# Earlier selections, more product buffers and more empty steps in a two-layer convolution kernel

## The reference, cut to what matters

```python
# layer 0: local attention over 3 x 3 neighbours, 4 heads of 64 channels
qkv = einsum('oc,bchw->bohw', w_qkv, gn(x));  q, k_, v = split(qkv, 3)
logits = einsum('bhdl,bhdkl->bhkl', q, patches(k_))            # 9 per pixel and head
attn_out = einsum('bhkl,bhdkl->bhdl', softmax(logits, axis=2), patches(v))
kernel = einsum('hkc,bhcl->bhkl', w_kg_g, cat) + b_kg          # 9 dynamic weights
conv_out = einsum('bhkl,bhdkl->bhdl', kernel, patches(v))
x = x + einsum('oc,bchw->bohw', w_proj, alpha * conv_out + beta * attn_out)
# layer 1: modulated deformable 3 x 3 convolution
om = conv3x3(gn(x), w_off) + b_off                             # offsets and masks
v = bilinear samples of gn(x) at each pixel, for 9 taps, times sigmoid(mask)
x = x + einsum('bckhw,ock->bohw', v, w)
```

## Time and profile before

| | us |
|---|---|
| median of 3 runs | 5400.81 (5400.7 to 5404.68) |
| the profiled execution | 5390.38 |
| its span, first to last instruction | 5388.6 |
| PE busy | 4889.6 (91%) |
| DVE busy | 4392.5 (82%) |
| ACT busy, POOL busy | 2297.6 (43%), 2282.9 (42%) |
| mean granted clock of PE | 0.972 of full speed |

### The profile page before, as it was taken

One profiled execution on the slowest core, in us unless ns is written; L12 is line 12 of the kernel. 1 busy time (PEld: TensorE's weight loads), 2 busy tenths in 40 slices (PEclk: granted clock), 3 DMA queues, 4 the chain that ended last, 5 costly groups with the idle time before them and its releaser, 6 DMA issues. The chain is left out here.

```text
span 5388.6 us, 80437 instructions
## 1 busy us (share of the span) xinstructions
PE 4889.6 (91%) x26816; PEld 2678.9 (50%) x26816; DVE 4392.5 (82%) x11212; ACT 2297.6 (43%) x5430; POOL 2282.9 (42%) x2311
## 2 busy tenths in 40 slices
PE   7868999999989998999989999899998989988888
PEld 4435554555545555455544555445554555544443
DVE  5656888878887888878888788888888878898998
ACT  2234444344443443534445344343444444443554
POOL 0003444444453444434444444444444344454776
PEclk9979999999999999999999999999999999999999
DMA  4326778877798777977779777887778877788999
GB/s 162 122 93 208 271 248 291 304 250 264 247 318 285 251 266 245 337 269 259 257 251 338 250 258 256 277 315 250 275 254 292 297 252 263 251 305 308 387 398 353
DMA packets 493125, 1451.51 MB, mean 269 GB/s; under 512 B 47396, under 2 KB 117420, under 8 KB 492460
## 3 DMA queue, kind: packets, MB, share of 16 engines
q0 software_dynamic: 331776, 1208.11, 64.3%
q1 hardware_dynamic: 160940, 238.27, 12.6%
HBM read 1309.60 MB, written 136.59 MB: 268 GB/s over the span
## 5 line engine op out<-in xcount | busy, mean ns | idle before, releaser
L730 POOL DMA_INDIRECT G<-table,IDX x2304 | 2282.0, 990 | 3066.6 <-DVE V L1381 2269.6
L749 PE MATMUL ps<-VT,s_wconv 128*128 128x512 f32 x4608 | 2277.5, 618 | 39.7 <-DVE R L1165 39.7
L1381 DVE SCALAR_TENSOR_TENSOR V<-G,WT,V 128x256 f32<-128x256 f32 x4608 | 2019.1, 479 | 122.6 <-DVE V L1381 3.2
L1109 ACT ACTIVATE VT<-ps 128x512 f32<-128x512 f32 x1152 | 686.0, 595 | 2390.0 <-PE ps L955 2387.9
L749 PEld LDWEIGHTS ps<-VT,s_wconv 128*128 128x128 f32 x4608 | 828.7, 194 | 871.7 <-issue 836.1
L1374 DVE SCALAR_TENSOR_TENSOR V<-G,WT 128x256 f32<-128x256 f32 x2304 | 1006.5, 477 | 84.0 <-ACT G L1098 40.1
L1129 DVE TENSOR_TENSOR E<-ps,s_band 128x512 f32<-128x512 f32 x1024 | 649.5, 682 | 455.3 <-PE ps L811 273.3
L955 PEld LDWEIGHTS ps<-s_ident,V 128*128 128x128 f32 x4608 | 574.5, 143 | 755.8 <-issue 754.5
L1098 ACT ACTIVATE G<-G,WT 128x256 f32<-128x256 f32 x1850 | 841.2, 499 | 111.0 <-DMA G<-table,IDX 110.1
L955 PE MATMUL ps<-s_ident,V 128*128 128x128 f32 x4608 | 708.8, 277 | 86.4 <-DVE V L1381 84.4
L787 PE MATMUL ps<-XN,s_wqk 128*128 128x512 f32 x1024 | 490.1, 606 | 14.8 <-ACT XN L1011 14.6
(11 more groups left out here) (101 smaller groups left out, 2764.9 us busy)
## 6 DMA issues: line engine op xcount, KB each, us to landing
table<-E SPq DMA_DIRECT2D x384, 176.0 KB
G<-table,IDX POOLq DMA_INDIRECT x2304
X<-in_x SPq DMA_DIRECT2D x64, 512.0 KB, 7.3
x<-X SPq DMA_DIRECT2D x64, 512.0 KB, 7.0
R<-x SPq DMA_DIRECT2D x64, 512.0 KB
out<-R SPq DMA_DIRECT2D x64, 512.0 KB, 5.8
G<-in_x SPq DMA_DIRECT2D x56, 512.0 KB, 4.4
s_wconv<-in_wconv SPq DMA_DIRECT2D x1, 2304.0 KB, 9.2
```

The costliest lines, as they stand in the source:

```text
L730: e.indirect_dma_start(G[a % NG][:, :], None, T[b % 2], bass.IndirectOffsetOnAxis(ap=IDX[b % 2][:, col:col + 1], axis=0)).then_inc(d_g[a % ...
L749: mm = e.matmul(CV[oh][:, :], s_wconv[:, h, t, oh * P:(oh + 1) * P], VT[U % 2][:, h, :], start=(t == 0 and h == 0), stop=(t == 8 and h == 1))
L1109: e.activation(VT[U % 2][:, :, 2 * P * pair:2 * P * (pair + 1)], BK[banks.place[use]][:, :].rearrange("p (h n) -> p h n", h=2), ACT.Copy). ...
L1381: e.scalar_tensor_tensor(vt[:, :], gt[:, q * C:(q + 1) * C], wt[:, col, q:q + 1], vt[:, :], ALU.mult, ALU.add).then_inc(lerp[q - 1], 1)
```

## The change

- `NE_BUF` goes from 4 to 6 (each buffer is 128 x 1024 float32, 4 KB per partition).
- `scores`: `hop(COLLECT)`, three empty steps, instead of one ahead of `ext`; and `hop(TURN)`, two, between `lg.out` and `lt`.
- `mix`: the first heads' `sel` waits only for x1 of chunk c - 1; the second heads' `sel` waits for the logits of chunk c + 1; both pairs of `sel` come before the first `pv`, and each `pv` has `hop(1 + alone)` ahead of it.
- `IDX` and `WT` become one tile each for nine chunks (`NW` = 9), addressed by `column(b, c, i, t)`; `w.mix` waits for the blending nine chunks back, from the tenth chunk on.
- the small tile `row` moves into a part of `G[3]`.

```diff
-NE_BUF = 4
+NE_BUF = 6
+NW = 9
+COLLECT, TURN = 3, 2
@@ def scores
-        yield IDLE
+        yield from hop(COLLECT)
         yield ("ext", b, c)
         have_logits.add((b, c))
         yield ("lg.out", b, c)
+        yield from hop(TURN)
         yield ("lt", b, c)
@@ def mix
-        while c > 0 and (b, c - 1) not in have_x1 or c + 1 < NCH and (b, c + 1) not in have_logits:
+        while c > 0 and (b, c - 1) not in have_x1:
             yield IDLE
         for hp in range(2):
+
+            while hp == 1 and c + 1 < NCH and (b, c + 1) not in have_logits:
+                yield IDLE
             for of in (OWN, BORDER):
                 yield ("sel", b, c, of, hp)
-            yield from hop(2 + alone)
+        for hp in range(2):
+            yield from hop(1 + alone)
             yield ("pv", b, c, hp)
@@ tiles
-        row = sb("row", [1, 72])
-        IDX = [sb(f"IDX{i}", [P, 32 * 9], U32) for i in range(2)]
-        WT = [sb(f"WT{i}", [P, 32 * 9, 4]) for i in range(2)]
+        IDX = sb("IDX", [P, NW * 36], U32)
+        WT = sb("WT", [P, NW * 36, 4])
+        row = G[3][0:1, 216:288]
@@ new
+        def column(b, c, i, t):
+
+            return 36 * ((b * NCH + c) % NW) + 9 * i + t
@@ w.mix
-                    if b > 1:
-
-                        e.wait_ge(lerp[2], 2 * PAIRS * (b - 2) + 36 * (c + 1))
+                    if b * NCH + c >= NW:
+
+                        e.wait_ge(lerp[2], 36 * (b * NCH + c - NW + 1))
```

More of the change, by code:

```diff
@@ L719, in _ @@
                         a = 2 * PAIRS * b + n
-                        col = (4 * c + i) * 9 + t
+                        col = column(b, c, i, t)
                         if n == 0:
@@ L731, in _ @@
                             G[a % NG][:, :], None, T[b % 2],
-                            bass.IndirectOffsetOnAxis(ap=IDX[b % 2][:, col:col + 1], axis=0)).then_inc(d_g[a % NG], 16)
+                            bass.IndirectOffsetOnAxis(ap=IDX[:, col:col + 1], axis=0)).then_inc(d_g[a % NG], 16)
         @block.tensor
@@ L1095, in _ @@
                         a = 2 * (b * PAIRS + m) + i
-                        col = (4 * c + 2 * pair + i) * 9 + t
+                        col = column(b, c, 2 * pair + i, t)
                         e.wait_ge(d_g[a % NG], 16 * (a // NG + 1))
                         e.activation(G[a % NG][:, 0:C], G[a % NG][:, 0:C], ACT.Copy,
-                                     scale=WT[b % 2][:, col, 0:1]).then_inc(act_scale, 1)
+                                     scale=WT[:, col, 0:1]).then_inc(act_scale, 1)
                 elif kind == "turn" and s[2] >= 0:
@@ L1313, in _ @@
                     lv = pg[:, :, :].rearrange("p t (k s) -> p t k s", s=2)
-                    idv = IDX[b % 2][:, 36 * c:36 * c + 36].rearrange("p (t k) -> p t k", t=4)
-                    wv = [WT[b % 2][:, 36 * c:36 * c + 36, q].rearrange("p (t k) -> p t k", t=4) for q in range(4)]
+                    at_w = column(b, c, 0, 0)
+                    idv = IDX[:, at_w:at_w + 36].rearrange("p (t k) -> p t k", t=4)
+                    wv = [WT[:, at_w:at_w + 36, q].rearrange("p (t k) -> p t k", t=4) for q in range(4)]
                     e.wait_ge(wts, at + 3)
@@ L1353, in _ @@
                     M = b * PAIRS + m
-                    wt = WT[b % 2]
-                    pairs = [(2 * M + i, G[(2 * M + i) % NG], V[(2 * M + i) % NV], (4 * c + 2 * pair + i) * 9 + t) for i in range(2)]
+                    pairs = [(2 * M + i, G[(2 * M + i) % NG], V[(2 * M + i) % NV], column(b, c, 2 * pair + i, t)) for i in range(2)]
                     for a, gt, vt, col in pairs:
@@ L1360, in _ @@
                                 e.wait_ge(wts, WTS * (b * NCH + c + 1))
-                            e.tensor_scalar(gt[:, 0:C], gt[:, 0:C], wt[:, col, 0:1], None, ALU.mult).then_inc(dve_scale, 1)
+                            e.tensor_scalar(gt[:, 0:C], gt[:, 0:C], WT[:, col, 0:1], None, ALU.mult).then_inc(dve_scale, 1)
                     if M > 2:
@@ L1373, in _ @@
                             e.wait_ge(dve_scale, count)
-                        e.scalar_tensor_tensor(vt[:, :], gt[:, C:2 * C], wt[:, col, 1:2], gt[:, 0:C],
+                        e.scalar_tensor_tensor(vt[:, :], gt[:, C:2 * C], WT[:, col, 1:2], gt[:, 0:C],
                                                ALU.mult, ALU.add).then_inc(lerp[0], 1)
@@ L1380, in _ @@
                                 e.wait_ge(lerp[1], a)
-                            e.scalar_tensor_tensor(vt[:, :], gt[:, q * C:(q + 1) * C], wt[:, col, q:q + 1], vt[:, :],
+                            e.scalar_tensor_tensor(vt[:, :], gt[:, q * C:(q + 1) * C], WT[:, col, q:q + 1], vt[:, :],
                                                    ALU.mult, ALU.add).then_inc(lerp[q - 1], 1)
```

## The result

The changed kernel takes 5243.01 us (median of 4 runs, 5240.78 to 5245.9) against 5401.32 before: a ratio of 0.9706, 95% interval 0.9693 to 0.9719. That is 158 us less where 184 were forecast.

What follows compares the result with a forecast made beforehand. PE was taken to bound all but the last 399 us. 204 us of its gaps gone, less 35 of new waits, plus 15 from the clock, net 184: 5400.8 to 5217 us, range 5150 to 5335.

Steps and rivals of the forecast that it cites:

- Gone: PE's waits at `pv`, `ext`, `lt` and for copied weights, middle and image 0's front: 204 us removed.
- New waits: Some PE gaps come back as waits for DVE's lerps: 5 us per image, 35 us in all.
- rival (a): The gaps come back because DVE is the real second bound: net gain 90 us, 5311 us; chance 0.22.
- The clock: Between 415 and 4990 us, fewer PE gaps return some of the 91 us missing to the clock: 15 us.
- rival (b): The clock between 415 and 4990 us returns whole, 91 us instead of 15: 5141 us; chance 0.08.
- Part 1: Three empty steps ahead of `ext` put at least one more `turn` between: 53 of 59.1 us gone.
- Part 3: Selections ahead of the first `pv`: 60 us gone in the middle, 30 in image 0's front, 8 at copied weights.
- parts 1 and 2: Empty steps ahead of `ext`, 53 us gone, and ahead of `lt`, 50 us gone plus 3 in image 0's front.
- Part 4: Six product buffers are exactly enough, none asked for while all are held: cost 0.
- Part 6: The longer list of steps, 64 on 2904 (2.2%), squeezes the offset phase: taken as 0, with 0 to 21 us.

Runs made afterwards that it cites:

- e3: The change with one empty step ahead of `ext` instead of three: 0.9732 of the kernel before.
- e8: The change with one empty step ahead of `ext` and none ahead of `lt`, keeping moved selections and buffers: 0.9775 of the kernel before.
- e2: The change with selections back behind the next chunk's logits, each `pv` right behind its own, both spacings kept: 0.9898 of the kernel before.
- e9: The change with four product buffers, first heads' selections held for the next chunk's logits, four selections then two `pv`: 0.9699 of the kernel before.
- e7: e6 plus one empty step between the second heads' selections and two ahead of chunk 6's first selection: 5296.61 us, 0.9601 of the kernel before.
- e6: The change with one empty step added ahead of each `ot` step: 0.9691 of the kernel before.
- e1: The kernel before's list of steps with only the change's memory side (six buffers, nine-chunk tiles, moved `row`): 5506.26 us, 0.9987 of the kernel before.
- e4: The change with no empty step between `lg.out` and `lt` instead of two: 0.9720 of the kernel before.

## Why the prediction was right, and which terms were off

The mechanism held: the gain is PE's idle time at `pv`, `ext` and `lt`, and the last convolution is untouched (398.5 us). DVE's share in layer 0 rose as forecast, if less: between the first gathers behind 1050 and 1512 us of the earlier trace rows it was busy 83% of the time, and between the same two gathers now 384.7 of 445.7 us, 86%, where I had 88. Term by term, from the traces of the pair:

- **Gone, 204 forecast, 216 measured.** In the middle `pv` 59 (60), `ext` 52 (53), `lt` 55 (50), copied weights 12 (8); in the front of image 0 `pv` 36 (30), `lt` 4 (3), `ext` -2 (0).
- **New waits, 35 forecast, 84 measured** (216 less the 132.0 that idle time fell). This is the step that was mis-sized: the term of 35. I put all of it at the lerps and reasoned from DVE's load. The lerps took 9.9 us in the middle (37.5 to 47.4); ot took 23.4, the banks of the selections 27.2, the norm 6.3, and the rest is small. Between 415 and 4850 us the lerp waits were 57.8, just below the 60 to 110 that I named, so rival (a) did not come in its form.
- **The clock, 15 forecast, 15.5 measured in busy time**, but at another place. I looked for it in the middle, where no busy time came back; the front of image 0 gave 14.9. That the sum has the right size here is luck.
- **The page rule on the clock.** The Trainium skill, "TensorE: Matmul & The Clock Gate", section "A second HAM failure mode: psum-queue depth-cycling", has short idles between groups of matmuls as what makes the clock swing. Taken fully, as in rival (b), it would have given back the whole 91 us. The pair doesn't show that: the idle time of the middle fell by a third with the clock still at 0.98.
- **Part 1's reason was wrong, its sum right.** I wrote that one more turn is enough and that DVE makes the products before the next lerp. Where a lerp stands between the last two `s` it doesn't, and the one turn behind them doesn't cover that: 34 of 34 such places wait in e3. Three empty steps work because they leave no such place with a single turn (and raise the places with two turns or more from 7 to 28).
- **Part 3 was undervalued, parts 1 and 2 overvalued.** By waits I had 98 for part 3 and 106 for parts 1 and 2. On the chip part 3 alone, with its buffers, is worth 2.25% (e8), 122 us by ratio, and the spacings add 0.88% to it, 48 us; alone they bring 1.0% (e2), since most of what they remove at `ext` and `lt` comes back at `pv` while `pv` stands right behind its products.
- **Part 4** cost nothing, as forecast, but what it allows is not needed either (e9).
- **Part 6, the longer list, at 0**, was blind to its real effect. The added weight moves every step of the front against the 18 pairs of a convolution chunk. It doubled the places in which `ot` has no turn behind `om.out`, from 24 to 46, and the waits followed, 24 to 46. I could have counted this ahead: for `lt` of the kernel before the list has 42 such places, and the earlier trace rows have 42 waits.

The median moved by 158 and the span by 147.5 because the profiled execution of before was some 11 us faster than its median, much as the prediction had it.

Left open: why the shift by 6 of weight is worth some 23 us in one kernel and 54 in the other. No run takes one group away with all else in place, and none of these edits could.

## What to carry to other kernels

Where all engines walk one metered list, count for each pair of dependent steps what lies between them, and in which order; the count is to be had before a run. For `ot` and `lt` the places with nothing between were nearly the waits (24 and 24, 46 and 46, 42 and 42, 35 and 33). It is not the whole: `ext` waited in 34 of the 48 places of e3 that had one turn, and in e7 `lt` waited 14 times, 23.6 us, with one such place in the list. The waits also don't add up to the gain: 59.4 us taken away at `ot` were worth nothing (e6), and the moved selections were worth 122 us where their waits promised 98 (e8). An edit worth under 1% could not be told here from the shift that it gives to all the other steps; try the shift by itself (here one constant, worth 0.4% and 1.0%). Try the new order with the old buffers too: four product buffers did what six did (e9), and six with the old order brought nothing (e1).

## What was not expected of the hardware

Less idle time of PE doesn't always bring back its clock, and can come with less of it. In the middle of the pair 101 us of idle time went with no change in busy time. On one chip, from e3 to e4, 47 us went (295.4 to 248.7) and 45 us of busy time came for it, with the clock at 0.97 instead of 0.98:

```profile
395.42:4859.20 4463.78, 4168.34 (x23247) 2294.41 (x23244) 3729.73 (x9621) 1936.28 (x4619) 1950.63 (x1994) 0.98 0.79 274
```

```profile
390.69:4853.20 4462.51, 4213.80 (x23252) 2313.43 (x23248) 3734.04 (x9629) 1932.45 (x4620) 1963.03 (x1994) 0.97 0.79 274
```

And e7 has nearly the idle time of e4 (251.5 us) with a clock of 0.99 and 4154.5 us of busy time. So the sum of PE's idle time does not tell the clock; what does is not shown here.

The kernel before took 5401 us in the first pair and 5505 to 5514 on the three chips of the experiments, 2% more, while the change's ratio is 0.9706 and 0.9687, with overlapping intervals.
